# A two-layer language-model tower on one core: set-up steps, normalisation, context, causal mask and the first ternary layer rearranged

## The chip, the core and the metric

The kernel runs on one core of one Trainium2 chip. A core has five engines with instruction lists of their own: PE (TensorE, matrix products), DVE (VectorE), ACT (ScalarE), POOL (GpSimd) and SP (SyncE, which here only issues DMAs). They wait for one another through semaphores. SBUF is the on-chip memory of 128 partitions, PSUM the memory of eight banks into which TensorE writes. The metric is device time in microseconds.

## The reference

The input is 16 sequences of 128 tokens, hidden size 256, 16 heads of 16 features. Layer 0 embeds and normalises the tokens, applies attention with random features and then a low-rank mixture of prototypes. Layer 1 is causal attention with rotary embedding and a ternary feed-forward part. In short:

```
x  = layernorm(word[ids] + pos[types] + type[mask]) * gamma + beta
# layer 0, attention: 44 random features a head
td = (t * dn) @ proj.T
qp = ratio * (exp(td_q - diag_q - rowmax) + EPS)
kp = ratio * (exp(td_k - diag_k - max over keys and features) + EPS)
context = einsum('bhnm,bhnd->bhmd', kp, v)
out = einsum('bhmd,bhnm,bhn->bhnd', context, qp, 1 / (qp @ kp.sum))
h  = relu((out @ Wo.T + bo) @ Wfc.T + bfc), added to the stream
# layer 0, feed-forward: the two nearest of 32 prototypes, rank 16 each, gated
# layer 1, attention
q, k = rope(h @ Wq), rope(h @ Wk)
a  = softmax(causal(q @ k.T / 4)) @ v @ Wo
# layer 1, feed-forward: ternary weights
Wt = clip(round(W / (mean|W| + 1e-5)), -1, 1)
y  = relu(n(h) @ W1t.T + b1) @ W2t.T + b2
```

Every sublayer is fed a layernorm of the stream and added to it.

## The kernel before

One tile is one sequence (128 tokens on the partitions). There are 16 tiles, and each goes through some 90 named steps. A step is one or a few instructions on one engine, and it is written once, in that engine's `step(op, t)`. There is no loop over tiles in the usual sense: `due(engine)` sorts all (step, tile) pairs of an engine by a planned time, computed from `START`, `STRETCH` and `PLACE`, and the engine runs the sorted list in that order. About six to eight tiles are in flight: TensorE has issued the first product of tile 7 before the last one of tile 0. On TensorE the function `free` adds waits for the readers of a PSUM bank before the bank is written again.

Matrices are kept as a 16-bit upper part and a 16-bit lower part. `split_product` sums three products for each of the two halves of the contraction (L1320). Five layernorms a tile carry the letters E, P, F, R, M. For each, DVE makes the statistics (`Est`, `Eag` and so on), POOL raises to the power -1/2 (`Ers`, L539 and its like), DVE makes the negated mean times that (`Enm` L768, `Pnm` L785, `Fnm` L886, `Rnm` L956, `Mnm` L1018), and ACT normalises (`Exn` ..., L1075).

Steps that matter here, with their lines:

- *Start.* POOL writes constants (L601 to L626), gathers embedding rows (`g`, L521), adds them (`e2`, L535), scales and shifts (`esc` L542, `eh` L545). DVE fixes the ids first and writes padding (L1044 to L1062).
- *Set-up.* Loaded weights are split: ACT makes the upper part (L1078), DVE the lower (L659). These pieces are blocks inside the step of some tile: for example `setup_r` and `lower_rows("m")` stand behind `hg` of tile 0, `setup_f2` and `setup_masks` behind `on` of tile 0, and `quantise` (L749, L751), which makes the ternary weights, behind `kd` and `on` of tiles 1 and 2. The loads of later weights stand behind `qT` and `qp` of tile 0 on SP.
- *Context.* `ctx` (L1487) multiplies the key features of two heads (88 fp32 columns) with the values of two heads. The products across the two heads are not wanted: `ctxt` (L843) multiplies in PSUM by `pair_mask`, `cth` (ACT) and `ctl` (L846) split the result, and `o` (L1508) applies it to the queries. `kbc` (L1472) spreads the keys' maximum to all partitions.
- *Causal attention.* `mk1` and `mk2` (L1382) each write a mask of 0 and -1e30 into four PSUM banks: four matmuls of the identity with 512 columns. `s1` (L1737) adds the 16 heads' scores with tokens on partitions, `ngm` (L987) takes the negated row maximum, and `s2` (L1758) makes the transposed scores with the maximum as one more contraction row. `ex1` and `ex2` take the exponential and `pvx` (L1771) multiplies with the values, four heads side by side in the array's columns. Each score matmul has 48 rows of contraction of a head's 64 slots in `s1`, 64 in `s2`.
- *Feed-forward, layer 1.* `m1` (L1862, L1863) has tokens on partitions: eight matmuls of 512 columns and two for the bias. `mh1`, `mh2` (ACT, L1309, L1305) and `ml1`, `ml2` (DVE, L1030, L1026) split the result into `ms`, which lies over `stage_r`. It is transposed by a DMA (`mT`) for tiles 0 to 14, and on TensorE (`mTp` L1830, then `mTa`, `mTb`) for tile 15. `m2` (L1878, L1879) is the last product, `ob` (L1035) adds it to the stream and `st` stores it.

## Time and profile before

| | |
|---|---|
| three runs, us | 479.64, 479.53, 477.95 (median 479.53) |
| profiled execution (its time is known as its span) | 481.0 us |
| instructions | 11690 |
| PE, weight loads (PEld) | 82%, 56% of the span |
| DVE, ACT, POOL | 76%, 57%, 52% |
| mean granted TensorE clock | 0.929 of full speed |
| DMA moved | 56.47 MB |

All times in rows are microseconds from the start of the span unless ns is said. A row of a group reads: line, engine, operation, written tile `<-` read tiles, shapes, count, then busy time and the mean length of one in ns, then idle time of the engine just before and what ended it. A matmul row such as `128*88 128x34` has a stationary operand of 128 rows and 88 columns and streams 34 columns. Matmuls are pipelined: a run of equal ones is shorter than the sum of their lengths. An fp32 matmul is recorded twice.

### The profile page before, as it was taken

The numbers are of one execution on the slowest core, as the hardware profiler recorded it, in microseconds if no ns is written. First come the engines' busy times: TensorE is split into PE (matmuls) and PEld (weight loads), VectorE is DVE, ScalarE is ACT, GpSimd is POOL, SyncE is SP. The second block draws the span as 40 slices with busy tenths as digits, with TensorE's granted clock in tenths as the row PEclk, the third lists the DMA queues.
The fourth block names the chain that finished last, engine by engine and source line by source line (L and its number), as shares of the span: only waits on it lengthen the run. The fifth ranks groups of instructions, "written<-read, shape, count | busy, mean of one in ns | idle before, by whom it ended". The sixth has DMA issues, their size and how long they took to land. (4 is left out here: it accounts for less than half of the span.)

```text
span 481.0 us, 11690 instructions
## 1 busy us (share of the span) xinstructions
PE 395.6 (82%) x3871; PEld 268.2 (56%) x3901; DVE 367.2 (76%) x1009; ACT 273.6 (57%) x589; POOL 248.1 (52%) x334
## 2 busy tenths in 40 slices
PE   3263665787887899999999999999999989888876
PEld 1132443554555656667575757575757666565634
DVE  4466689988868888889888879798889786674552
ACT  1234673454747575858484857667575846455431
POOL 6883432565655656566666766656645434142000
PEclk9767557779989999999999999999999998999999
DMA  3928823043845657587989796979786963722223
GB/s 112 229 84 256 195 34 68 12 89 59 143 86 116 103 114 126 121 145 123 144 145 165 116 165 123 167 115 165 114 162 114 163 118 79 146 45 46 57 56 76
DMA packets 176908, 56.47 MB, mean 117 GB/s; under 512 B 168432, under 2 KB 174224, under 8 KB 176848
## 3 DMA queue, kind: packets, MB, share of 16 engines
q1 hardware_dynamic: 175216, 51.25, 57.3%
q0 software_dynamic: 1632, 4.46, 3.9%
q8 instruction: 32, 0.52, 0.5%
q14 instruction: 28, 0.23, 0.1%
HBM read 11.98 MB, written 2.36 MB: 30 GB/s over the span
## 5 line engine op out<-in xcount | busy, mean ns | idle before, releaser
L987 DVE TENSOR_REDUCE split<-PS 128x16 f16<-128x2048 f32 x16 | 36.8, 2297 | 5.9 <-PE PS L1737 5.6
L586 POOL TENSOR_TENSOR stage_f<-stage_f 128x512 f32<-128x512 f32 x16 | 20.2, 1265 | 33.4 <-DVE stage_f L965 27.3
L1075 ACT ACTIVATE xnR<-hres,nmeanR,rstdR 128x256 f32<-128x256 f32 x16 | 9.6, 600 | 43.7 <-DVE nmeanR L956 43.7
L1862 PE MATMUL PS<-w1q,xTM 128*128 128x512 f16 x128 | 32.8, 379 | 1.9 <-DMA xTM<-xsM 1.2
L1330 PE MATMUL PS<-proj_hi,qkT 128*128 128x176 f16 x128 | 24.3, 253 | 11.9 <-DMA qkT<-qs 9.1
L1878 PE MATMUL PS<-w2q,mT 128*128 128x256 f16 x256 | 30.6, 272 | 1.6 <-ACT mT L1072 0.9
L560 POOL TENSOR_TENSOR qe<-qef,qe 128x704 f16<-128x704 f32 x16 | 24.3, 1521 | 12.3 <-ACT qe L1165 12.3
L1878 PEld LDWEIGHTS PS<-w2q,mT 128*128 128x128 f16 x256 | 24.0, 98 | 5.9 <-issue 1.6
L1320 PE MATMUL PS<-wqkT_hi,xTP 128*128 128x512 f16 x64 | 24.5, 426 | 2.8 <-DVE proto_sq L683 2.5
L1620 PE MATMUL PS<-faT_hi,hgT 128*128 128x256 f16 x128 | 25.6, 288 | 1.3 <-DMA hgT<-hgs 0.8
L579 POOL TENSOR_TENSOR rstdR<-rstdR,consts 128x1 f32<-128x1 f32 x16 | 8.7, 546 | 33.3 <-DVE rstdR L952 33.3
L1075 ACT ACTIVATE ehat<-esum,nmeanE,rstdE 128x256 f32<-128x256 f32 x16 | 9.6, 598 | 28.4 <-DVE nmeanE L768 28.4
L1487 PEld LDWEIGHTS PS<-va,kp 128*88 128x88 f32 x256 | 24.0, 168 | 2.8 <-ACT kp L1172 0.6
L1072 ACT ACTIVATE split<-stage_f 128x256 f16<-128x256 f32 (+1 forms) x48 | 21.7, 477 | 5.2 <-POOL stage_f L586 4.7
L1331 PE MATMUL PS<-proj_lo,qkT 128*128 128x176 f16 x128 | 24.4, 253 | 0.0
L1487 PE MATMUL PS<-va,kp 128*88 128x34 f32 x256 | 23.9, 251 | 0.0
L1320 PE MATMUL PS<-rwqk_hi,xTR 128*128 128x512 f16 x64 | 21.8, 382 | 2.1 <-DVE xTR L960 1.4
L575 POOL TENSOR_TENSOR hgs<-hg,hgs 128x512 f16<-128x512 f32 x16 | 18.9, 1180 | 8.8 <-ACT hgs L1072 8.8
L1320 PE MATMUL PS<-fbT_hi,xTF 128*128 128x512 f16 x64 | 22.6, 394 | 0.0
L1330 PEld LDWEIGHTS PS<-proj_hi,qkT 128*128 128x128 f16 x128 | 13.2, 103 | 14.0 <-DMA qkT<-qs 10.3
L596 POOL TENSOR_TENSOR rstdM<-rstdM,consts 128x1 f32<-128x1 f32 x16 | 8.7, 542 | 23.7 <-DVE rstdM L1014 23.6
L555 POOL TENSOR_TENSOR xso<-onorm,xso 128x256 f16<-128x256 f32 x11 | 7.4, 670 | 26.0 <-ACT xso L1072 26.0
(324 smaller groups left out, 1405.5 us busy)
## 6 DMA issues: line engine op xcount, KB each, us to landing
out<-outb SPq DMA_DIRECT2D x16, 128.0 KB, 2.6
w<-in_w1T SPq DMA_DIRECT2D x1, 1024.0 KB
w<-in_w2T SPq DMA_DIRECT2D x1, 1024.0 KB
stage_p<-in_wqkT SPq DMA_DIRECT2D x1, 512.0 KB
stage_f<-in_fbT SPq DMA_DIRECT2D x1, 512.0 KB, 5.0
stage_f<-in_faT SPq DMA_DIRECT2D x1, 512.0 KB, 5.2
stage_r<-in_rwqk SPq DMA_DIRECT2D x1, 512.0 KB, 4.3
rT<-split SPq DMA_TRANSPOSE x26, 3.3
```

Source lines behind the costliest of these rows:

```text
L560: g.tensor_tensor(qel[:, :, 0:MP], pairs(qef), qeh[:, :, 0:MP], ALU.subtract).then_inc(qel_ok, 1)
L586: g.tensor_tensor(rot[:, :, :].rearrange("p h d -> p (h d)"), rc[:, :], rs[:, :], ALU.add).then_inc(rot_ok, 1)
L987: v.tensor_reduce(slots(48)[:, 0:H, 0].rearrange("p (c j) -> p j c", j=4), PS[:, BANK["mk1"]:BANK["mk1"] + 4, :].rearrange("p j (c k) -> p ...
L1072: return a.activation(dst, src, ACT.Copy)
L1075: a.activation(dst, src, ACT.Identity, bias=nmean[x][:, 0:1], scale=rstd[x][:, 1:2]).then_inc(xn_ok[x], 1)
L1320: last = pe.matmul(dst, xT[x][:, xp, :], wp[:, c, :], start=(n == 0), stop=(n == 3 * KC - 1 and bias is None))
L1330: pe.matmul(dst, qkT[:, c0 + c, :], proj_hi[:, :], start=True, stop=False)
L1331: last = pe.matmul(dst, qkT[:, c0 + c, :], proj_lo[:, :], start=False, stop=True)
L1487: last = pe.matmul(PS[0:MP, BANK["ctx"], 2 * VA * j:2 * VA * (j + 1)], kp[:, j * MP:(j + 1) * MP], va[:, 2 * j:2 * j + 2, :].rearrange("p ...
L1620: pe.matmul(PS[:, BANK["y"], 0:D], hgT[:, xp, :], wp[:, c, :], start=(c == 0 and xp == 0 and wp is whi["faT"]), stop=False)
L1862: pe.matmul(dst, xT["M"][:, n, :], w1q[:, n % KC, cols], start=(n == 0), stop=False)
L1878: pe.matmul(PS[:, BANK["m2"], 0:D], mT[:, j, :], w2q[:, j % FC, :], start=(j == 0), stop=False)
```

## The change

- *Order.* `due` no longer computes places. Each engine has a written list (`ORDER`), in which a step's n-th mention is its n-th tile. The warm-up products on TensorE and the choice of tiles that are turned by DMA stay.
- *Set-up apart.* The set-up blocks become pieces of their own in the lists (`zp1` ... `zq4` on DVE, `yp1` ... `ym3` on ACT, `xo1`, `xo2`, `xt` on TensorE, `lR`, `lW1`, `lW2` on SP). Scaling of the rope tables moves to the host. Constants other than the identity and the masks are written by DVE, ahead of its work on the ids; those left on POOL come ahead of its wait for the ids. In POOL's list the first steps are `g g e2 Ers esc e2 eh Prs Ers g e2 g` (before: `g g e2 Ers g esc e2 eh Ers Prs`).
- *Negated means.* The five `nmean` operations a tile move from DVE to POOL, right behind the power, with a wait for it.
- *Context.* Two heads get 64 feature slots each (128 instead of 88 columns), with zeros in the rest. `cth` and `ctl` read only the two diagonal blocks, each in two instructions of half the size, and apply the factor of `pair_mask`; `ctxt` and `pair_mask` go. `o` contracts over 128 rows.
- *Causal mask.* Scores come first in their banks. Up to 15 slots of a head that were empty now hold constants of +-6e4, which hide whole blocks of 32 tokens. Only the four diagonal 32 x 32 blocks of each bank get mask matmuls, behind the scores: 16 for `s1` and 16 for `s2`.
- *First ternary layer.* `m1` is written with features on partitions: 32 matmuls of 128 columns with the weights stationary, and the bias ahead of them, two matmuls of 64 rows. `mh` and `ml` write into `hidden` and `stage_r` in turn, and `m2` reads them there. `mT`, `mTp`, `mTa`, `mTb` go.

```
+                    g.wait_ge(rs_ok["R"], t + 1)
+                    g.tensor_scalar(nmean["R"][:, :], mv["R"][:, 0:1], rstd["R"][:, 1:2], -1.0, ALU.mult, ALU.mult)\
+                        .then_inc(nm_ok["R"], 1)
...
-                elif op == "ctxt":
-                    wait(v, ctx_ok, t + 1)
-                    ctxt = PS[0:MP, BANK["ctx"], 0:H * VA].rearrange("p (a b) -> p a b", a=HP)
-                    v.tensor_tensor(ctxt, ctxt, pair_mask[:, :, :], ALU.mult).then_inc(ctxt_ok, 1)
...
+                    for i in range(2):
+                        v.scalar_tensor_tensor(out=ctl[MS * i:MS * i + M, :, VA * i:VA * (i + 1)],
+                                               in0=diagonal(PS[:, BANK["ctx"], 0:H * VA], i), scalar=CS,
+                                               in1=cth[MS * i:MS * i + M, :, VA * i:VA * (i + 1)],
+                                               op0=ALU.mult, op1=ALU.subtract).then_inc(ctl_ok, 1)
...
+            for r in range(P // BLOCK - 1):
+                v.memset(queries[BLOCK * r:BLOCK * (r + 1), :, PARTS + FOLD * r:PARTS + FOLD * (r + 1)], HIDE).then_inc(pad_ok, 1)
+                v.memset(keys[BLOCK * (r + 1):BLOCK * (r + 2), :, PARTS:PARTS + FOLD * (r + 1)], -HIDE).then_inc(pad_ok, 1)
...
-            def masks(mask):
+            def hide(mask):
                 for j in range(4):
-                    pe.matmul(PS[:, BANK["mk1"] + j, :], ident_b[:, :], mask[:, :, :].rearrange("p c k -> p (c k)"),
-                              start=True, stop=False, skip_group_check=True)
+                    for r in range(P // BLOCK):
+                        block = slice(BLOCK * r, BLOCK * (r + 1))
+                        last = pe.matmul(PS[block, BANK["s1"] + j, :].rearrange("p (c k) -> p c k", c=4)[:, :, block],
+                                         ident_b[block, block], mask[block, block].unsqueeze(1).to_broadcast([BLOCK, 4, BLOCK]),
+                                         start=False, stop=True, skip_group_check=True, tile_position=(BLOCK * r, BLOCK * r))
+                return last
...
+                    for h in range(H):
+                        o = SLOT * (h % 2)
+                        pe.matmul(scores(h), rT[o:o + SLOT, HP + h // 2, :], rTm[o:o + SLOT, h // 2, :],
+                                  start=(h < 4), stop=False, skip_group_check=True)
+                    hide(mask_kq).then_inc(s2_ok, 1)
...
                     for b in range(2):
-                        dst = PS[:, BANK["m1"] + b, :]
-                        cols = slice(b * F1 // 2, (b + 1) * F1 // 2)
+                        pe.matmul(PS[:, BANK["m1"] + b, :], rows["m1"][0:BR, :], sel[:, 4 * b:4 * b + 4, :].rearrange("k c n -> k (c n)"),
+                                  start=True, stop=False, skip_group_check=True)
+                    for f in range(FC):
                         for n in range(2 * KC):
-                            pe.matmul(dst, xT["M"][:, n, :], w1q[:, n % KC, cols], start=(n == 0), stop=False)
-                        last = pe.matmul(dst, pick[:, :], rows["m"][:, cols], start=False, stop=True)
+                            last = pe.matmul(PS[:, BANK["m1"] + f // 4, f % 4 * P:(f % 4 + 1) * P], w1q[:, n % KC, f * P:(f + 1) * P],
+                                             xT["M"][:, n, :], start=False, stop=(n == 2 * KC - 1), skip_group_check=True)
                     last.then_inc(m1_ok, 1)
```

## Rows read from the trace of the kernel before

**Rows 1.** The page, busy us (share of the span) and instructions.
```profile
PE 395.6 (82%) x3871; PEld 268.2 (56%) x3901; DVE 367.2 (76%) x1009; ACT 273.6 (57%) x589; POOL 248.1 (52%) x334
```

**Rows 2.** Windows: stretch, its length, busy us by engine, clock, DMA share, GB/s.
```profile
64.00:112.00 48.00, 33.11 (x263) 22.46 (x263) 43.78 (x108) 21.73 (x51) 26.35 (x29) 0.73 0.27 54
203.60:409.40 205.80, 195.04 (x2061) 135.77 (x2078) 173.26 (x492) 137.28 (x306) 119.57 (x157) 0.99 0.80 136
```

**Rows 3.** Timeline (start, length, engine, line, operation): VectorE at the first output.
```profile
203.63 0.40 DVE L1035 SCALAR_TENSOR_TENSOR outb<-hres,PS 128x256 f32<-128x256 f32 x1
```

**Rows 4.** Timeline, TensorE, one tile's steps at full clock.
```profile
249.95 0.81 PE L1382 MATMUL PS<-mask_qk,ident_b 128*128 128x512 bf16 x3
250.69 0.62 PE L1737 MATMUL PS<-rT 48*128 48x128 f16 x16
...
259.38 0.39 PE L1472 MATMUL PS<-ident,kmx_row 16*128 16x16 f32 x2
259.83 1.08 PE L1771 MATMUL PS<-stage_p,vr 128*32 128x128 f32 x32
...
264.86 1.37 PE L1487 MATMUL PS<-va,kp 128*88 128x34 f32 x16
```

**Rows 5.** Groups by line and shape, TensorE (PE products, PEld weight loads).
```profile
L1487 PE MATMUL PS<-va,kp 128*88 128x34 f32 x256 | 23.9, 251 | 0.0
L1771 PE MATMUL PS<-stage_p,vr 128*32 128x128 f32 x512 | 18.1, 284 | 2.3 <-ACT stage_p L1271 1.7 <-issue 0.2
L1382 PE MATMUL PS<-mask_qk,ident_b 128*128 128x512 bf16 x48 | 12.9, 378 | 4.1 <-DVE rT L983 2.9 <-issue 0.5
L1737 PE MATMUL PS<-rT 48*128 48x128 f16 x256 | 10.0, 217 | 3.1 <-DMA rT<-split 3.1
L1472 PE MATMUL PS<-ident,kmx_row 16*128 16x16 f32 x32 | 6.5, 278 | 1.9 <-DVE kmx_row L827 1.9
L1771 PEld LDWEIGHTS PS<-stage_p,vr 128*32 128x32 f32 x512 | 14.0, 113 | 3.8 <-issue 3.4
```

**Rows 6.** Groups by line and shape, VectorE.
```profile
L843 DVE TENSOR_TENSOR PS<-PS,pair_mask 88x272 f32<-88x272 f32 x16 | 7.0, 436 | 2.2 <-PE PS L1487 2.2
L956 DVE TENSOR_SCALAR nmeanR<-mvR,rstdR 128x1 f32<-128x1 f32 x16 | 3.4, 211 | 1.6 <-POOL rstdR L579 1.6
```

**Rows 7.** Groups by line and shape, GpSimd.
```profile
L579 POOL TENSOR_TENSOR rstdR<-rstdR,consts 128x1 f32<-128x1 f32 x16 | 8.7, 546 | 33.3 <-DVE rstdR L952 33.3
L572 POOL TENSOR_TENSOR hgs<-gates,hgs 128x32 f16<-128x32 f32 x16 | 3.9, 245 | 5.6 <-ACT hgs L1072 5.5
```

**Rows 8.** Timeline of the first 32 us.
```profile
8.19 0.31 POOL L610 MEMSET fbias<- 32x256 f32 x1
...
11.71 0.98 POOL L521 DMA_INDIRECT hres<-in_word,ids  x1 [0.16 <-issue]
...
20.76 1.77 POOL L542 TENSOR_TENSOR escaled<-ehat,gamma 128x256 f32<-128x256 f32 x1
...
31.65 0.58 PE L1320 MATMUL PS<-wqkT_hi,xTP 128*128 128x512 f16 x1 [2.49 <-DVE proto_sq L683]
```

**Rows 9.** Timeline, VectorE: the steps on both sides of `setup_r` and `lower_rows("m")`.
```profile
77.13 0.69 DVE L922 SCALAR_TENSOR_TENSOR hg<-PS,gates 128x512 f32<-128x512 f32 x1
...
83.47 0.42 DVE L932 COPY hgT<-PS 128x512 f16<-128x512 f16 x1
```

**Rows 10.** The chain that ended last: start, length, what.
```profile
459.15 0.60 ACT stage_r L1309
...
459.78 0.69 DVE stage_r L1030
...
467.64 4.26 DMA mT<-stage_r
...
476.37 1.92 PE PS L1878 x16
```

**Rows 11.** Timeline, TensorE: the turn of the last tile, 16 blocks of 128 columns.
```profile
474.15 1.05 PE L1830 MATMUL PS<-ident_h,stage_r 128*128 128x128 f16 x16
```

More of the change, by code:

```diff
@@ L150, in taken, with made @@
     return op not in FOR_DMA or t not in BY_PE[FOR_DMA[op]]
-def due(engine):
-    def place(op, t):
-        return START[t] + STRETCH[t] * PLACE[op][0 if t < FIRST else 2 if t >= LAST else 1]
-    return sorted(((op, t) for op in ENGINE[engine] for t in range(TILES) if taken(op, t)), key=lambda x: (place(*x), x[1]))
-TURNS = {x: n + 1 for n, x in enumerate(y for y in due("PE") if y[0] in ("rT3p", "mTp", "rT1p", "rT2p", "hgTp",))}
+ONCE = {
[7 rows of a table added]
+}
+def due(engine):
+    seen = {}
+    for op in ORDER[engine].split():
+        tiles = [0] if op in ONCE[engine] else [t for t in range(TILES) if taken(op, t)]
+        n = seen[op] = seen.get(op, -1) + 1
+        yield op, tiles[n]
+def made(engine, piece, part=None):
+    count = 0
+    for op, _ in due(engine):
+        if op == piece:
+            return count + (ONCE[engine][op] if part is None else part)
+        count += ONCE[engine].get(op, 0)
+    raise KeyError(piece)
+TURNS = {x: n + 1 for n, x in enumerate(y for y in due("PE") if y[0] in ("rT3p", "rT1p", "rT2p", "hgTp"))}
 def wait(eng, sem, count):
@@ L972, in step @@
                 elif op == "rc":
+                    if t == 0:
+                        v.wait_ge(load["R"], 16 * 5)
                     wait(v, rqk_ok, t + 1)
@@ L1106, in setup_m, with upper_matrix @@
-            def setup_m():
-                a.wait_ge(load["M"], 16 * 3)
-                a.wait_ge(v_set, 10)
-                junk = wneg[:, :].bitcast(F16)
-                for k, w in enumerate((w1, w2)):
-                    a.wait_ge(a_set, 13 + k)
-                    a.activation(junk, w[:, :], ACT.Abs, accum_out=absum[:, k:k + 1]).then_inc(a_set, 1)
-                upper(rows["m"][0:BR, :], row["m"][:, :], 1.0)
+            def upper_matrix(src, k):
+                upper(whi[k][:, :, :], src[:, :, :], WS)
@@ L1171, in step @@
                     wait(a, ctx_ok, t)
-                    a.activation(kp[:, :], ke[:, :], ACT.Identity, bias=FEATURE_EPS).then_inc(kp_ok, 1)
+                    a.activation(kp[:, :, 0:M], by_feature(ke), ACT.Identity, bias=FEATURE_EPS).then_inc(kp_ok, 1)
                 elif op == "cth":
-                    wait(a, ctxt_ok, t + 1)
+                    wait(a, ctx_ok, t + 1)
                     wait(a, o_ok, t)
-                    copy(cth[:, :, :], PS[0:MP, BANK["ctx"], 0:H * VA].rearrange("p (a b) -> p a b", a=HP)).then_inc(cth_ok, 1)
-                    if t == 0:
-                        setup_r()
+                    for i in range(2):
+                        a.activation(cth[MS * i:MS * i + M, :, VA * i:VA * (i + 1)], diagonal(PS[:, BANK["ctx"], 0:H * VA], i),
+                                     ACT.Copy, scale=CS).then_inc(cth_ok, 1)
                 elif op == "oe":
```

986 lines of the change are left out of this document (531 added, 455 removed), and 39 rows, old and new, of tables (BANK, BY_PE, FOR_DMA, FOR_PE).

## The prediction, made before the changed kernel was run

> **What bounds the kernel now.** I read the page first: TensorE's matmul side is busy 82% of the span [rows 1]. Such averages hide stages, so next I read busy time by stretch, with stretches cut at events [rows 2]. The first output eviction is at 203.6 and the tenth at 409.4: nine tiles in 205.8 us, 22.87 us a tile. TensorE is busy 195.0 of them at full clock, VectorE 173.3 [rows 2, 3]. This stage is TensorE's. From 64 to 112 VectorE is busy 43.8 of 48.0 us and TensorE 33.1, at a mean clock of 0.73 [rows 2]: there VectorE's list is the limit, because one-off set-up stands between the steps of the first tiles [rows 9]. Before 31.65 TensorE has no tile's product at all [rows 8]. At the end I read the chain of waits: a DMA of 4.26 us and turns stand between the last products [rows 10].
>
> TensorE's records overlap, so I count pitches: (length of a run of n equal matmuls minus one of them) over n-1.
>
> **Part 1, the start.** *Gathers and constants.* Today GpSimd writes constants from 8.19 on, between the first tile's gathers and the second's (11.71), issues the second's, and only then makes the first sum; the third tile's gathers stand ahead of `esc` at 20.76 [rows 8]. Afterwards the constants are VectorE's (14 memsets, ahead of the ids) or come ahead of the ids on GpSimd, so the second tile's gathers and the sum move up by 11.71 - 8.19 = 3.5 us, and `esc` has no gather ahead of it: two of about 1 us each. `esc` of tile 0 also takes 1.77 us, beside a VectorE split; if the split moves, 1 us goes. VectorE's extra memsets can delay the ids a little, and the padding memsets delay the warm-up, where TensorE has no work yet. The first product needs the q/k weights too; their DMAs are released by the same event as now, and no row shows when they land. I take 7 us off 31.65. Bounds: 3.5 (the gathers alone) and 9.
>
> *Set-up apart.* Nothing of it but the rope scaling is removed; each piece gets a place of its own. Today 6.3 us of set-up stand between the gated product of tile 0 (77.13) and VectorE's next step of a tile (83.47) [rows 9], and the steps behind them queue. Ahead of tile 0's negated maximum (`ngm`), today's list has 14 negated means and three `ctxt`, which go: 14 x 0.21 + 3 x 0.44 = 4.2 us [rows 6]. Rope scaling, narrower masks and a shorter row add an estimated 1.9; three split `ctl` take 0.5 back. VectorE is contiguous there, so about 6 us. The moved pieces can as well land ahead of something urgent (in the new list three stand between `kd` and `ctl` of tile 0, a fourth just ahead of `kd`), so the bounds are 1 and 9. Start in all: 13 us, bounds 4.5 and 18.
>
> **Part 2, TensorE per tile.** *Causal mask.* Eight 512-column matmuls with the full identity go. Their pitch is (0.81-0.38)/2 = 0.216 us, so 1.73 us [rows 4, 5]. In come 32 matmuls of 32 rows, 32 weight columns and 128 moving columns, on the four diagonal blocks of the array. The extra contraction rows that hide whole blocks ride inside the score matmuls at no cost: 16 of those take 0.62 at 48 rows [rows 4], and their number and columns stay. No row shows a diagonal block. Nearest: the half-height scores, two side by side, pitch (0.62-0.22)/15 = 0.027, and the quarter-width `pvx`, four side by side, (1.08-0.28)/31 = 0.026 a record, fp32 [rows 4, 5]. I take 0.027: 0.86 us, a saving of 0.87. Lower bound, four abreast, 0.0135: saves 1.30. Upper bound, one at a time, (1.05-0.22)/15 = 0.055 as in the last turn [rows 11]: 1.76, no saving. Beyond that lies rival C.
>
> The Trainium skill speaks against the saving. Its page "TensorEngine Tiling (Array Packing)", section "Gotcha 1: PSUM Pressure", says that different row tiles cannot write the same PSUM bank at the same time. Here four do; today's score pairs go to different banks. By it the masks would cost the upper bound, which is rival B.
>
> *Context.* A head's features get 64 slots, not 44, so `ctx` loads 128 fp32 weight columns, not 88. Its pitch today is (1.37-0.25)/15 = 0.075 for 34 moving columns, more than `pvx` needs for 128, so the load sets it. The `kbc` matmul loads 128 fp32 columns for 16 moving ones: two in 0.39 with 0.28 each, a pitch of 0.11 [rows 4, 5]. Cost 16 x (0.11-0.075) = 0.57 us; bounds 0 and 0.57.
>
> The Trainium skill agrees: "TensorE: Matmul & The Clock Gate", section "LDWEIGHTS (loading the stationary operand)", has the load grow with weight columns and not with rows.
>
> *First ternary layer.* Eight 512-column matmuls of 0.216 become 32 of 128 at 0.055 [rows 11], 1.73 to 1.76; the two bias matmuls stay. The features land on partitions, so the transposed copy `mT` (15 DMAs, one turn on TensorE) disappears.
>
> Per tile -0.87 + 0.57 + 0.03 = -0.27; over 16 tiles -4 us, bounds -20 (masks four abreast, context free) and +10 (masks singly, context dear).
>
> **Part 3, the other engines.** VectorE loses five negated means (1.05) and `ctxt` (0.44) a tile and gains at most 0.2 for `ctl` in two halves: -1.3 us [rows 6]. GpSimd gains five small operations, each between the 0.25 of `gsl` and the 0.55 of its power [rows 7]: 1.3 to 2.8 us a tile, on an engine that is idle half of the time; its place in line is that of the power. Queued behind it are `esc`, `Plo`, `qel`; ScalarE's normalisation waits for it, up to 0.4 later than today, hidden while TensorE has other tiles. ScalarE gets `cth` twice, 0.2. Of TensorE's 10.8 idle us in the nine tiles [rows 2] some are waits for VectorE; its freed time and a new order can close or open gaps. I take -2 over the run, from -8 to +5. The `mT` DMAs free queue time that nobody waits for before the end: nothing.
>
> **Part 4, the end.** Today the last product starts at 476.37: ahead of it stand tile 14's DMA (4.26 from 467.64), its product, a turn of 16 blocks and its copies [rows 10]. The last first layer has run by about 471.4, since tile 14's product follows the DMA at once. Afterwards a ScalarE eviction (0.60) and two VectorE ones (0.69 each, overlapping by a little) lead from it to the product, as they lead to the DMA today: 0.60 + 2 x 0.69 = 2.0 [rows 10]. So 473.5, 2.9 earlier. Masks on the chain give 0.5, the mean on GpSimd takes some back. -3, bounds -1 and -5.
>
> **Sum.** The profiled span is 481.0; the median of the three runs is 1.5 less. 481.0 - 13 - 4 - 2 - 3 = 459.0, less 1.5 = **457.5 us**. Start and end carry 16 of the 22.
>
> **Rivals.**
> A. *The start keeps only the gathers' part* (4.5 instead of 13): the moved set-up stands ahead of the first tiles' chain. 466. For it: the four pieces named above, and on ScalarE three matrix splits ahead of tile 0's `ke`. Against: VectorE's list is shorter whatever its order.
> B. *Mask matmuls run singly*, being in one bank: 0.90 us a tile more than taken, 457.5 + 14 = 472. Against: they differ in output partitions as well, and `pvx` shares its bank.
> C. *The slow side: the small blocks' weight loads don't hide, or the array empties at each change of shape.* A load of 32 columns is recorded at 0.113 us in `pvx`, hidden there [rows 5]. At that a matmul the masks cost 3.6 a tile, 2.75 more than taken: 457.5 + 44 = 502. It makes the kernel slower than now from 22/16 = 1.4 us more than taken, that is from 2.25/32 = 0.07 us a matmul. Against: `pvx` and the scores hide theirs.
> D. *Masks four abreast and gaps closing:* 457.5 - 7 - 6 = 444.
>
> **How the numbers follow.** Forecast (448 to 465) 0.56, A 0.14, B 0.14, C 0.08, D 0.05, and 0.03 that the new order costs what the rest gives (about 480). The range takes in D and B, with a margin for A and B in part together: 443 to 476. A measurement of this kernel tells about 0.5% from no change. Faster by more: 0.86; within: 0.05; slower: 0.09.
>
> **What would show it.** First q/k product near 24; `ngm` of tile 0 near 99 instead of 112; outputs 22.4 to 22.7 apart; 16 mask matmuls in about 0.4 us behind 16 scores; 16 `ctx` records in about 1.9 instead of 1.37; the last product about 2 us behind the last first layer. The prediction is wrong if the outputs are 22.9 or more apart, or the first comes no earlier than 195.

## The result and the profile after

The changed kernel takes 488.0 us (median of five runs, 483.2 to 489.6) beside 478.2 for the kernel before (five runs, 475.8 to 479.6): a ratio of 1.021, 95% interval 1.017 to 1.025. The prediction was 457.5 us, range 443 to 476, and both signs that it named for being wrong are there: outputs 22.9 or more apart (23.12) and a first output no earlier than 195 (205.1). It has the wrong sign. Ratios are formed without executions of a slower state, which matters for e16 at the end of the table: it stands on four of ten, and over all ten it would be 1.014. The span of the profiled execution, 481.3 us, is the shortest of the five and hardly differs from that before (481.0), so I read the parts of the profile first and then a second profile of the same kernel (span 488.5, on another chip, where the ratio was 1.015).

The line of busy times of the page of the kernel after, and then its busy time by stretch (columns as in [rows 2]):

```profile
PE 395.1 (82%) x4653; PEld 288.2 (60%) x4653; DVE 353.6 (73%) x947; ACT 275.8 (57%) x605; POOL 270.8 (56%) x401
```

```profile
64.00:110.00 46.00, 35.56 (x271) 23.71 (x269) 38.21 (x91) 25.93 (x57) 26.55 (x32) 0.72 0.29 58
205.10:413.20 208.10, 191.61 (x2470) 144.02 (x2468) 164.90 (x446) 139.39 (x315) 125.41 (x190) 0.99 0.64 111
413.20:481.30 68.10, 55.04 (x747) 41.14 (x747) 36.16 (x89) 28.99 (x59) 13.24 (x22) 1.00 0.12 31
```

From the first output (205.10) to the tenth (413.18) lie 208.1 us, 23.12 a tile, where it was 22.87 [rows 2, 3]. TensorE is busy 191.6 us of it, not 195.0: its work did fall, by 0.38 us a tile. But it stands idle 16.5 us instead of 10.8. VectorE is busy 164.9 instead of 173.3 and GpSimd 125.4 instead of 119.6. Both moved the way that the change says (VectorE by 0.93 us a tile where 1.3 was forecast, GpSimd by 0.65 for 1.3 to 2.8), and the tiles came no closer.

Times from the trace, kernel before against kernel after:

| | before | after |
|---|---|---|
| first q/k product | 31.65 | 25.42 |
| first negated maximum | 112.1 | 110.4 |
| first output | 203.6 | 205.1 |
| tenth output | 409.4 | 413.2 |
| last output | 478.4 | 478.8 |

The way from the first negated maximum to the first output, in which the pipeline fills, took 94.7 us instead of 91.5. The prediction did not look at this stretch by itself, and it costs more than the nine tiles behind it (3.2 against 2.3 us).

TensorE's timeline of the kernel after, one tile at full clock (columns: start, length, engine, line, operation and tiles, form, count). L1825 is the first score products, L1458 the block masks, L1847 the second score products, L1859 `pvx`, L1579 `ctx`, L1930 and L1934 the bias and weights of `m1`:

```profile
251.86 0.62 PE L1825 MATMUL PS<-rT 63*128 63x128 f16 x16
252.41 0.40 PE L1458 MATMUL PS<-mask_qk,ident_b 32*32 32x128 bf16 x16
252.75 0.28 PE L1392 MATMUL PS<-rwv_hi,xTR 128*128 128x256 f16 x1
...
258.80 0.62 PE L1847 MATMUL PS<-rTm,rT 64*128 64x128 f16 x16
259.35 0.40 PE L1458 MATMUL PS<-mask_kq,ident_b 32*32 32x128 bf16 x16
...
261.93 1.08 PE L1859 MATMUL PS<-stage_p,vr 128*32 128x128 f32 x32 [0.23 <-issue]
...
264.67 1.95 PE L1579 MATMUL PS<-va,kp 128*128 128x34 f32 x16
266.45 0.63 PE L1873 MATMUL PS<-ident,stage_f 128*128 128x128 f32 x4
...
268.31 0.60 PE L1930 MATMUL PS<-sel,rows_all 64*128 64x512 f16 x2
268.85 1.96 PE L1934 MATMUL PS<-xTM,w1q 128*128 128x128 f16 x32
270.64 0.24 PE L1402 MATMUL PS<-proj_hi,qkT 128*128 128x176 f16 x1
```

The prices of the sum can be read off. The 16 masks keep TensorE from 252.41 to 252.75, 0.34 us: twice that is 0.68 a tile, less than the 0.86 I took and half-way to the lower bound. `ctx` lasts 1.95 where 1.9 was forecast. From its start to the next step are 1.78 us; before, 1.20 (264.86 to 266.06; its record is in [rows 4]). `m1` takes 268.31 to 270.64, 2.33 us; before it was ten records at a pitch of 0.216, 2.16: +0.17 where I took +0.03. Together -1.05 + 0.58 + 0.17 = -0.30 against a forecast of -0.27 and a measured fall of 0.38.

The rows show one more thing, which the sum did not hold. The second scores start 6.94 us behind the first (258.80 - 251.86) and `pvx` 3.13 behind them. In the kernel before the same tile's `pvx` starts at 259.83, 9.14 behind the first scores [rows 4]; now it is 10.07.

What TensorE waited for in the nine tiles of the kernel after (waiting line, releaser, us in total, times, longest):

```profile
PE PS L1392 <- DMA xTo<-xso: 2.0, 4, 0.9
PE PS L1551 <- DVE kmx L883: 2.0, 3, 1.0
PE PS L1564 <- DVE kmx_row L887: 1.8, 4, 0.5
PE PS L1859 <- ACT stage_p L1343: 1.8, 3, 0.7
PE PS L1825 <- DMA rT<-split: 1.6, 2, 1.3
```

No single wait has appeared. The idle time is spread over a dozen of them, each below 1.4 us.

### The profile page after: what moved, and what is told of

Its sections match the earlier page's. It is cut to its first block, busy times and chain, and to the rows that moved or that the text cites. A ratio compares the mean times of both kernels' runs of the same rounds, so it can differ in the third digit from the quotient of the medians.

```text
span 481.3 us, 13220 instructions
## 1 busy us (share of the span) xinstructions
PE 395.1 (82%) x4653; PEld 288.2 (60%) x4653; DVE 353.6 (73%) x947; ACT 275.8 (57%) x605; POOL 270.8 (56%) x401
## 4 chain that ended last, share of the span: by engine, by line
PE 43%; issue 12%; DVE 12%; POOL 11%; DMA 10%; ACT 7%; SPq 3%; ACTq 0%; POOLq 0%; DVEq 0%
PE PS L1392 12%; PE PS L1579 4%; PE PS L1934 4%; DMA rT<-split 4%; PE PS L1859 3%; PE PS L1952 3%; DMA xTo<-xso 2%; PE PS L1710 2%; DMA hgT<-hgs 2%; PE PS L1458 1%; SPq L508 1%; POOL emb L566 1%; PE PS L1930 1%; PE PS L1402 1%; POOL split L656 1%
## 5 line engine op out<-in xcount | busy, mean ns | idle before, releaser
L1579 PE MATMUL PS<-va,kp 128*128 128x34 f32 x256 | 33.7, 290 | 3.4 <-ACT kp L1246 3.3
L1579 PEld LDWEIGHTS PS<-va,kp 128*128 128x128 f32 x256 | 33.2, 208 | 5.3 <-ACT kp L1246 4.5
L1934 PEld LDWEIGHTS PS<-xTM,w1q 128*128 128x128 f16 x512 | 28.6, 98 | 6.8 <-issue 6.8
L1934 PE MATMUL PS<-xTM,w1q 128*128 128x128 f16 x512 | 31.4, 219 | 0.0
L1710 PE MATMUL PS<-faT_hi,hgT 128*128 128x256 f16 x128 | 27.4, 300 | 1.9 <-DMA hgT<-hgs 1.4
L1392 PE MATMUL PS<-rwqk_hi,xTR 128*128 128x512 f16 x64 | 23.2, 405 | 0.4 <-DVE xTR L1003 0.3
L1133 ACT ACTIVATE ehat<-esum,nmeanE,rstdE 128x256 f32<-128x256 f32 x16 | 9.5, 593 | 21.9 <-POOL nmeanE L593 21.1
L656 POOL TENSOR_TENSOR split<-stage_f,split 128x512 f16<-128x512 f32 x16 | 18.5, 1155 | 5.5 <-ACT split L1130 5.4
L1859 PE MATMUL PS<-stage_p,vr 128*32 128x128 f32 x512 | 17.6, 278 | 3.4 <-ACT stage_p L1343 1.8
L566 POOL DMA_INDIRECT hres<-in_word,ids x16 | 16.9, 1054 | 5.8 <-DVE ids_pt L1103 2.9
L1392 PE MATMUL PS<-wvT_hi,xTP 128*128 128x256 f16 x64 | 14.6, 294 | 6.5 <-DVE wvT_lo L716 6.5
```

Of the source, the lines that this page charges most:

```text
L566: g.indirect_dma_start(dst, None, table, bass.IndirectOffsetOnAxis(rows_, 0)).then_inc(g_ok[slot], 16)
L656: g.tensor_tensor(slots(32), rot[:, :, :], slots(16), ALU.subtract).then_inc(rl_ok, 1)
L1392: last = pe.matmul(dst, xT[x][:, xp, :], wp[:, c, :], start=(n == 0), stop=(n == 3 * KC - 1 and bias is None))
L1579: last = pe.matmul(PS[:, BANK["ctx"], 2 * VA * j:2 * VA * (j + 1)], kp[:, 2 * j:2 * j + 2, :].rearrange("p h m -> p (h m)"), va[:, 2 * j:2 ...
L1710: pe.matmul(PS[:, BANK["y"], 0:D], hgT[:, xp, :], wp[:, c, :], start=(c == 0 and xp == 0 and wp is whi["faT"]), stop=False)
L1859: last = pe.matmul(PS[32 * j:32 * (j + 1), BANK["pvx"], c * P:(c + 1) * P], vr[:, 4 * c + j, :], pfull[:, j, c, :], start=True, stop=True)
```

## The experiments

The lists of both kernels hold the same tile steps, so orders and parts can be exchanged. For the runs on the **old order** the place function of the kernel before was evaluated, its steps written out as lists, and the set-up pieces put behind the steps that carried them before. Each ratio is to the kernel before on the same chip. Spacing is the mean distance of outputs one to ten in the profile, busy is TensorE's time in these nine tiles over nine, idle the rest.

| run | ratio (95% interval) | spacing | busy | idle |
|---|---|---|---|---|
| before (its own profile) | 1 | 22.87 | 21.67 | 1.20 |
| after | 1.021 (1.017 to 1.025) | 23.12 | 21.29 | 1.83 |
| e1 after, again | 1.015 (1.011 to 1.019) | 23.48 | 21.17 | 2.31 |
| e2 old order | 1.037 (1.032 to 1.041) | 23.75 | 21.39 | 2.37 |
| e3 old order, new set-up | 1.071 (1.066 to 1.075) | 23.71 | 21.39 | 2.32 |
| e4 new order, old set-up | 1.034 (1.028 to 1.041) | 23.49 | 21.33 | 2.16 |
| e5 e2 + means on VectorE | 1.020 (1.013 to 1.026) | 23.21 | 21.16 | 2.05 |
| e6 e2 + old masks | 1.007 (1.003 to 1.011) | 23.27 | 22.10 | 1.17 |
| e9 e2 + small masks ahead | 1.013 (1.008 to 1.017) | 23.30 | 21.56 | 1.74 |
| e7 e6 + means + 108 columns | 0.997 (0.993 to 1.001) | 22.89 | 21.93 | 0.96 |
| e10 e7, both masks small | 1.005 (1.001 to 1.009) | 23.29 | 21.51 | 1.77 |
| e13 e7, first mask small | 1.001 (0.996 to 1.005) | 22.67 | 21.38 | 1.29 |
| e14 e7, second mask small | 1.004 (1.001 to 1.008) | 23.27 | 21.76 | 1.50 |
| e17 e13, half of GpSimd's work | 0.996 (0.993 to 0.999) | 22.84 | 21.55 | 1.30 |
| e18 e13, half of the maximum | 0.996 (0.993 to 0.999) | 22.25 | 21.35 | 0.90 |
| e8 after, 108 columns | 1.007 (1.003 to 1.011) | 22.92 | 21.02 | 1.90 |
| e11 after, means on VectorE | 1.020 (1.011 to 1.030) | 23.25 | 21.28 | 1.97 |
| e12 after, small masks ahead | 1.012 (1.007 to 1.017) | 23.20 | 21.30 | 1.90 |
| e15 after, start moved | 1.010 (1.003 to 1.018) | | | |
| e16 e12 + 108 columns + start | 1.005 (0.999 to 1.011) | | | |

The profiled execution of e15 took 490.4 us beside 482.9 to 484.8 for its four others, and that of e16 485.4 beside a median of 484.4, so only the order of events is read in them. e17 and e18 leave out work and are no candidates.

### Order or work (e1 to e4)

My first theory was that the new lists had lost what the new work gained; the rival was that the new work itself opens the gaps.

e1, the changed kernel again:

> The changed kernel itself, for comparison with the three orders beside it. From its five times, 483.2 to 489.6 us, median 488.0, a ratio to the kernel before of about 1.02. Its own profile (span 481.3) stands at the low end of its times; this look is to show where the other runs lose some 5 us more: if it is one stall, one stretch between outputs is longer than in the first profile; if it is many gaps, the nine tiles from the first to the tenth output take 210 to 213 us rather than 208.1.

Measured 1.015; the nine tiles took 211.3 us, spread as expected. The longest distances between outputs stand at the same places in both profiles (the third, 25.1 and 26.1 us, and the seventh, 26.3 and 26.2); the first six together are longer in e1 by 3.6 us. The same kernel's spacing differs by 0.36 us between the two profiles, so below the ratios decide, and a spacing from one profile only supports them.

e2, old order, all the new work:

> All of the changed work (masks by rows and blocks, means on GpSimd, wide context, feature-major layer), but each engine's tile steps in the order of the kernel before, and the set-up pieces behind the same steps as before. Theory ORDER (the new lists lose what the new work gains): 461 to 470 us, outputs 22.4 to 22.8 us apart, first output near 198. Theory WORK (a part of the new work, such as the wait for GpSimd's mean or the wide context, opens TensorE's gaps whatever the order): 480 to 490, outputs 23.0 or more apart.

```
-ORDER = { ... the new lists ... }
+ORDER = { ... the kernel before's steps in its order, set-up behind the steps that held it ... }
```

Measured 1.037, 500.6 us, outputs 23.75 apart. ORDER fell: the new lists are better for the new work than the old ones are, by 2%. It is not one stage: the first output comes at 212.5 instead of 208.8 (e1), and the outputs are 0.27 us further apart.

e3 and e4 exchange the places of the set-up only:

> As the run with the old order, but the set-up pieces stand where the new lists have them (ahead of the same or a neighbouring tile step). If the new place of the set-up is what costs the start, this is slower than the old order by 3 to 6 us, with the first context product of tile 0 near 52 as in the changed kernel; if the place of the set-up is worth the 6 us that the prediction gave it, it is faster by 3 to 6.

> The changed kernel with its tile steps in the new order, but the set-up pieces behind the same steps as before. Under the theory that the set-up's new place costs: 482 to 485 us. Under the theory that the order of the tile steps costs: within 1% of the changed kernel, 485 to 493, and outputs still 23 us or more apart.

Both lost: 1.071 from 1.037, and 1.034 from 1.015. The first negated maximum came at 129.6 instead of 113.0, and at 121.2 instead of 114.5. A place of the set-up is worth up to 3% of the run, but neither place is better in itself. Each fits its own tile order. Part of it can be the clock: TensorE was granted its lower level, 1.2 GHz, for 85.1 us ahead of the first maximum in e3 and for 51.6 in e2, for 69.9 in e4 and for 62.4 in e1.

### The parts, on the old order (e5, e6, e7)

e5 takes the negated mean out of GpSimd's steps and puts it at its old place in VectorE's list:

```
-                    g.wait_ge(rs_ok["R"], t + 1)
-                    g.tensor_scalar(nmean["R"][:, :], ...)
+    "DVE": ... Rag hP Pst Rnm ...
```

> The old-order run (500.6 us beside a kernel before of 482.4, outputs 23.75 us apart) with the five negated means a tile back on VectorE at their old places. If the wait for GpSimd's second operation is what spreads the outputs: about 485 us. If the cause is elsewhere: within 3 us of 500.6, or slower by up to 5, since VectorE gets 1.05 us a tile back.

Measured 1.020 from 1.037, although VectorE got the five means back (its busy time rose by 0.58 us a tile, from 167.9 to 173.1 us in the nine tiles; GpSimd's fell by 1.27). On that order GpSimd was the worse place for the means. Most of the gain lies ahead of the nine tiles: the first output comes at 202.4 instead of 212.5.

e6 puts four full mask matmuls ahead of the scores, as own steps, in place of the blocks behind them:

```
-                    hide(mask_qk).then_inc(s1_ok, 1)
+                elif op == "mk1": ... 4 x matmul(identity, 128 x 512) ...
+                elif op == "s1": ... scores only ...
```

> The old-order run with the four 512-column mask matmuls ahead of the scores at their old places, in their own steps, and none of the block masks (the hiding rows hold zeros, so the result is the same). TensorE gets about 1.0 us a tile of work back. By the sum of TensorE's work this is slower than 500.6 by up to 16 us. If it is the masks behind the scores, on the way from scores to the negated maximum and to the exponentials, that hold the tile up, with four banks held meanwhile, it is no slower or faster: 485 to 500.

Measured 1.007 from 1.037: the kernel became 3% faster with 0.7 us a tile more to do on TensorE (22.10 busy for 21.39). This is the opposite of what the sum of TensorE's work says. Here too more than half lies ahead of the first output (201.0 instead of 212.5), and part can be the granted clock, of which more below.

e7 has both, and a context product of 108 columns:

```
-                        ... kp[:, 2 * j:2 * j + 2, :]  (128 columns)
+                        ... kp[:, 2 * j:2 * j + 2, :] ... [:, 0:MS + M]  (108 columns)
```

> The old-order run with three parts back: means on VectorE, old masks, and 108 instead of 128 weight columns in the context product (rows 108 to 127 of its output are read by nobody). If these three are what differs in effect from the kernel before, about 482 to 486 us. If it stays near 500, the cause is in what is left: the feature-major first layer with its later release of banks, the context split in halves, or the changed start.

Measured 0.997: as fast as the kernel before. So on the old order the three parts together make the loss; what is left (feature-major layer, context in halves and 20 columns wider, the start's constants) sums to nothing that can be measured. That they make it on the new order too is not shown by this; e8, e11 and e12 ask it.

### The place of the masks and their size (e9, e10, e13, e14)

> The old-order run with the small block masks issued ahead of the scores, as steps at the old masks' places, and the hiding rows kept: only the place of the masks differs from the old-order run (1.037 of the kernel before), only their shape and the hiding rows from the run with the old masks (1.007). Theory PLACE (masks behind the scores lengthen the way from scores to maximum and exponentials and leave TensorE nothing to do in its waits): 1.007 or less, by up to 1.0 us a tile of TensorE's work, 466 to 482 us. Theory SHAPE (the small blocks themselves disturb): stays near 1.037, 496 us.

e9 has the small blocks of the changed kernel, but issues them ahead of the scores (`start=True` in the blocks, `start=False` in the scores). Measured 1.013 from 1.037: PLACE accounts for most of the 3% that e6 gave back. In the trace the maximum starts 0.60 us behind the start of the last score product in e2 and 0.27 in e9 (mean of tiles 5 to 13), and the exponentials 0.60 and 0.27 behind the last second score. In the kernel before they are 0.28 and 0.26. Behind the scores, each group of masks stands on the way of its own tile, for 0.33 us. But e9 is not faster than e6 (1.007), which has 0.54 us more TensorE work.

> As the run before it, and means on VectorE and 108 weight columns. The same with the old masks took 0.997 of the kernel before. Theory PLACE: 0.965 to 0.99, 461 to 474 us, since 1.0 us a tile of TensorE's work goes. If TensorE's work no longer sets the time there: 0.997.

Measured 1.005: with cheaper masks than e7 it is, if anything, slower. Here are the nine tiles of e7, then of e10, then of e13, and behind them the stretch from the first maximum to the first output in e7 and in e10 (columns as in [rows 2]):

```profile
196.10:402.10 206.00, 197.36 (x2295) 146.64 (x2294) 173.04 (x492) 140.67 (x315) 119.84 (x158) 1.00 0.65 114
```

```profile
201.50:411.10 209.60, 193.63 (x2520) 144.64 (x2516) 172.80 (x493) 139.96 (x315) 119.79 (x158) 0.98 0.64 111
```

```profile
197.40:401.40 204.00, 192.40 (x2396) 144.60 (x2394) 173.10 (x492) 139.93 (x315) 119.97 (x158) 1.00 0.64 115
```

```profile
108.70:196.10 87.40, 78.67 (x894) 56.29 (x892) 75.34 (x221) 60.44 (x137) 52.52 (x67) 1.00 0.59 110
109.90:201.50 91.60, 79.83 (x986) 57.06 (x987) 75.67 (x221) 60.61 (x137) 52.53 (x67) 0.95 0.66 105
```

TensorE can be busy 197.4 us of 206.0 at full clock. With 3.7 us less to do, it needs 209.6. So its work at full clock did not set the time in e10. But the granted clock there was 0.98 instead of 1.00, and ahead of the first output 0.95 instead of 1.00, and this is a rival to every explanation by waits. The time that TensorE stood at its lower level, 1.2 GHz, between the first maximum and the last output:

| | first maximum to last output, us | of it at 1.2 GHz, us |
|---|---|---|
| before | 366.3 | 6.8 |
| after | 368.3 | 10.2 |
| e1 | 371.4 | 5.8 |
| e2 | 383.2 | 20.1 |
| e6 | 365.5 | 3.0 |
| e9 | 368.5 | 12.9 |
| e7 | 360.3 | 0 |
| e10 | 368.9 | 23.3 |
| e13 | 362.1 | 9.6 |
| e14 | 367.3 | 13.7 |

What such time costs can be read at either level: `pvx` takes 1.94 us in e10 at 396.89, at the lower level, and 1.08 in [rows 4]. As an estimate from the two levels, a microsecond at 1.2 GHz loses at most half of itself. So e10 can owe the clock up to 11.7 us, more than the 8.6 by which it is longer than e7, and e14 up to 6.9 of its 7.0: waits and clock are not separated there. The ten executions of e10 say the same: the five shortest (478.5 to 480.2 us) were granted 0.928 to 0.936 of full speed in the mean, the five others (480.4 to 483.9) 0.915 to 0.922. Ahead of the fall at 396.0 in e10 TensorE had been busy 5.30 of 6.8 us. No run shows whether the saved work brings the fall about. Other differences are too large for the clock: e9 is 14.7 us shorter than e2, the clock can be 3.6 of it, and e6 is 17.7 shorter, the clock 8.6. And it does not explain the loss of the changed kernel, which in e1 stood at the lower level for less time than the kernel before.

e13 and e14 make one mask small and leave the other full:

> Old order, means on VectorE, 108 weight columns, masks ahead: the mask of the first scores as 16 small blocks, that of the second as four full matmuls. With both full the ratio was 0.997, with both small 1.005. Theory COVER (the stretch from first to second scores is as long as the maximum and a transposing DMA take, so that TensorE's work saved in it is lost, and only work saved outside it counts): 0.5 us a tile faster than both full, ratio 0.975 to 0.99, the stretch near 6.5 us, the rest of a tile near 13.1. If neither half counts: 0.997 to 1.005.

> The mirror of the run before: full masks ahead of the first scores, small ones ahead of the second. Theory COVER: no faster than both full (0.997), up to 1.5% slower, with the stretch from first to second scores near 7.2 us instead of 6.5 and TensorE idle over 1 us in it. If saved work counts wherever it is: the same as the run before.

Measured 1.001 and 1.004: neither half is worth anything that the times show. The theory COVER is half right at most. I cut each tile on TensorE at the first of the first scores, the first of the second scores and `pvx` (mean of tiles 5 to 12, which leave out the ends of the nine tiles, where e14 and most of e10 lose their clock; us, idle time in brackets):

| | first to second scores | to `pvx` | to the next first scores |
|---|---|---|---|
| before | 6.46 (0.37) | 2.86 | 13.71 (0.48) |
| e2 | 7.10 (1.40) | 3.21 | 13.62 (0.56) |
| e7 | 6.49 (0.40) | 2.88 | 13.67 (0.06) |
| e10 | 7.20 (1.40) | 3.00 | 13.03 (0.00) |
| e13 | 6.97 (0.86) | 2.86 | 13.10 (0.05) |
| e14 | 6.61 (0.93) | 2.88 | 13.65 (0.04) |
| after | 7.22 (1.01) | 4.36 | 12.38 (0.30) |

A cheap second mask (e14) leaves TensorE idle 0.5 us longer in the first stretch: as COVER says, the full mask had only filled a wait. A cheap first mask (e13) does shorten the last stretch, by 0.57 us. But then the first stretch is 0.48 longer, idle again. The saving becomes a wait, and the rows of what TensorE waited for from 200 to 400 us say for what, first in e13:

```profile
PE PS L1386 <- DMA xTo<-xso: 4.3, 6, 1.4
PE PS L1858 <- DMA rTm<-split: 2.3, 5, 0.7
```

In e7 no wait for `xTo` is listed, and that for `rTm` is as long:

```profile
PE PS L1850 <- DMA rTm<-split: 2.5, 2, 1.4
```

So it is not the operand of the second scores (`rTm`) that comes late in e13, but `xTo`, the transposed attention output of layer 0, which the product `of` in the same stretch needs. GpSimd makes its lower part and SP issues its DMA.

### What holds the tiles then (e17, e18)

> The run with the first mask cheap (ratio 1.001, outputs 22.67 us apart), with GpSimd's three longest operations (lower part of the query features, sum of the rotated halves, lower part of the gated product) halved in tiles 1 to 15; the other half of their outputs keeps old values. GpSimd loses about 2.0 us a tile. If GpSimd's list holds the tiles: the issue of the DMA for the second scores comes at once behind the maximum (0.47 us late before), the outputs come closer by 0.5 to 1.2 us, ratio 0.965 to 0.985. If not: ratio and spacing unchanged.

e17 leaves out half of GpSimd's three longest operations. Measured 0.996 from 1.001: 1.7 us less GpSimd work a tile (busy 104.7 for 120.0 us in the nine tiles) gave some 2 us in the whole run, with intervals that overlap. The wait for `xTo` fell from 4.3 to 1.9 us, and that for `rTm` rose from 2.3 to 4.4. GpSimd's list alone does not hold the tiles.

> The run with the first mask cheap, with the negated maximum taken for 8 of 16 heads in tiles 1 to 15 (the other heads keep the tile before's). The way from first to second scores gets 1.15 us shorter, and VectorE's list too. If that way holds the tiles: the stretch from first to second scores falls from 6.97 to about 6.1, where TensorE's own work of it ends, the outputs come closer by 0.8 us, ratio 0.96 to 0.975. If GpSimd's list or another holds them: the outputs stay 22.5 to 22.7 apart, and TensorE's idle time moves elsewhere.

e18 takes the maximum of 8 of the 16 heads only. Measured 0.996 too (against 1.001, again with overlapping intervals), with outputs 22.25 apart. The way from first to second scores was shortened by 1.07 us (2.30 to 1.23), and the stretch by 0.33 (6.97 to 6.64). The rows of one tile say why: SP's issues of the three transposing DMAs that stand together in its list (`onT`, `roT`, `rT3`), and VectorE's maximum, first in e13:

```profile
289.42 1.19 SPq L525 DMA_TRANSPOSE xTo<-xso  x1
289.54 2.30 DVE L1030 TENSOR_REDUCE split<-PS 128x16 f16<-128x2048 f32 x1
291.04 1.31 SPq L529 DMA_TRANSPOSE xTr<-xsr  x1
292.44 1.25 SPq L521 DMA_TRANSPOSE rTm<-split  x1
```

and in e18:

```profile
288.94 1.19 SPq L525 DMA_TRANSPOSE xTo<-xso  x1
289.06 1.23 DVE L1031 TENSOR_REDUCE split<-PS 128x8 f16<-128x1024 f32 x1
290.57 1.19 SPq L529 DMA_TRANSPOSE xTr<-xsr  x1
291.86 1.25 SPq L521 DMA_TRANSPOSE rTm<-split  x1
```

In e13 the maximum ends at 291.84 and `rTm` is issued at 292.44, when SP is done with `xTr` at 292.35. In e18 the maximum ends at 290.29, and the issue still comes at 291.86, behind `xTr` (291.76). An issue of a transposing DMA takes SP 1.2 to 1.3 us here, and `xTo` comes when GpSimd has made its lower part. In e7 (mean of tiles 5 to 13) the maximum ends 0.78 us after SP is done with the issue ahead, in e13 0.11 and in e18 0.85 before it. So I read one way (scores, maximum, DMA) as held by another (output of layer 0's attention, GpSimd, SP's queue) as soon as it gets shorter; no run moves `rTm` ahead in SP's list, which would test it.

The Trainium skill, page "TensorEngine Tiling (Array Packing)", section "Gotcha 1: PSUM Pressure", was weighed against the masks in the prediction; the trace does not bear it out here: four row tiles write one bank with a pitch of (0.40 - 0.22)/15 = 0.012 us, where one at a time had 0.055 [rows 11].

### The new order (e8, e11, e12)

> The changed kernel with 108 instead of 128 weight columns in the context product, the least that its slots allow. The pitch was 0.075 us at 88 columns and 0.111 at 128, so 16 records should take about 0.29 us a tile less: 4.6 us over the run if TensorE's work sets the time (485 us), nothing if waits set it.

Measured 1.007 against 1.015 for e1 (and 1.021 for the five runs): 0.8 to 1.4%, with 1.0 expected. The intervals of e8 and e1 just miss each other. Of TensorE's prices this is the one that shows in the time: twenty columns of the forty added are worth about 5 us.

> The changed kernel with the negated means back on VectorE, each at the place in VectorE's list at which GpSimd made it in the profile. In the old order this gave 1.7% back. If GpSimd's longer queue is the cause in any order: about 1.000 to 1.005 of the kernel before, 480 us. If the new lists have hidden it: no change from 1.015 to 1.021, or a little slower.

Measured 1.020 (1.011 to 1.030): no change from 1.015 to 1.021 that can be seen. The new lists seem to hide the means on GpSimd, which cost 1.7% on the old order.

> The changed kernel with the block masks ahead of the scores: for the first scores directly ahead of them, for the second three steps ahead (there they wait for the maximum). Theory PLACE: faster than the changed kernel by 1 to 3%. If the new lists have already fitted the rest around the masks behind: within 1% of it; slower if the earlier wait for the maximum now holds the three steps between.

Measured 1.012; the interval overlaps that of e1, so a gain of up to 1% is likely, not shown.

### The start (e15), and all together (e16)

In the kernel after, TensorE's first tile (timeline; in brackets idle time ahead and what ended it) and the step of ScalarE that held it:

```profile
25.42 0.58 PE L1392 MATMUL PS<-wqkT_hi,xTP 128*128 128x512 f16 x1 [1.49 <-DVE xTP L854]
...
36.80 0.40 PE L1392 MATMUL PS<-wvT_hi,xTP 128*128 128x256 f16 x1 [6.48 <-DVE wvT_lo L716]
...
41.80 0.31 PE L1402 MATMUL PS<-proj_hi,qkT 128*128 128x176 f16 x1 [2.37 <-DVE qd L875]
...
52.18 3.48 PE L1579 MATMUL PS<-va,kp 128*128 128x34 f32 x16 [3.13 <-ACT kp L1246]
```

```profile
34.63 0.60 ACT L1133 ACTIVATE ehat<-esum,nmeanE,rstdE 128x256 f32<-128x256 f32 x1 [5.43 <-POOL nmeanE L593]
35.13 0.61 ACT L1136 ACTIVATE wvT_hi<-stage_p 128x512 f16<-128x512 f32 x1
```

The first product is 6.2 us earlier than before, but the first context product, at 52.18, is 1.8 us later than the 50.34 of the kernel before. The split of the value weights stands behind the third tile's normalisation, which waits for its negated mean from GpSimd, behind that tile's gather.

```
-ACT: ... qhi0 Exn2 yp2 sq0 va0 ...         DVE: ... qlo0 Est2 Eag2 zm zo1 Pst1 Pag1 zp2 Est3 diag0 ...
+ACT: ... qhi0 yp2 sq0 Exn2 va0 ...         DVE: ... qlo0 zp2 Est2 Eag2 zm zo1 Pst1 Pag1 Est3 diag0 ...
```

> The changed kernel with three entries moved for tile 0: on ScalarE the upper part of the value weights and the squares ahead of the third tile's first normalisation, on VectorE the lower part of the value weights ahead of the third tile's statistics. In the profile ScalarE stood 5.4 us ahead of that normalisation and TensorE 6.5 us for the value weights. If this is what ate the start's gain: value product of tile 0 near 31 instead of 36.8, first negated maximum 3 to 5 us earlier than 110.4 to 114.5, time 1.010 of the kernel before instead of 1.018. If VectorE's list holds the start further on whatever comes in: the first negated maximum moves by under 1 us, time unchanged.

TensorE and then VectorE in e15:

```profile
31.27 0.27 PE L1398 MATMUL PS<-wvT_hi,xTP 128*128 128x256 f16 x1
...
43.23 0.30 PE L1408 MATMUL PS<-proj_hi,qkT 128*128 128x176 f16 x1 [9.11 <-DVE qd L881]
```

```profile
36.23 0.43 DVE L846 BATCH_NORM_STATS2 statsP<-hres 128x6 f32<-128x256 f32 x1 [2.21 <-POOL hres L609]
...
39.98 0.43 DVE L832 BATCH_NORM_STATS2 statsE<-esum 128x6 f32<-128x256 f32 x1 [2.93 <-POOL esum L593]
40.33 0.67 DVE L868 TENSOR_REDUCE diag<-sq 128x32 f32<-128x512 f32 x1
```

The value product came 5.5 us earlier, as the first theory said, and the next product of keys no earlier, as its rival said: VectorE stands at the statistics of tiles 1 and 3, which wait for GpSimd's sums, and tile 0's own steps are queued behind them. The first context product comes at 56.1, later than in both profiles of the changed kernel (52.2 and 55.3), and the first maximum at 113.7, between theirs. The time, 1.010, lies below 1.015 to 1.021, with intervals that overlap.

> The changed kernel with the small masks ahead of the scores (alone 1.012), 108 weight columns (alone 1.007) and the three moved entries. If they add up from 1.018: about 0.994, or 0.99 with the full gain of the start.

Measured 1.005 (0.999 to 1.011), where the single gains add up to 0.994. Its executions lie between 476.6 and 487.5 us, so this is the least certain value of the table. No version of mine is measurably faster than the kernel before and does all of its work; e7 comes closest.

## Why the prediction was wrong, step by step

Against the forecast of 22 us less, the two profiles miss by this much, stage by stage:

| | forecast | after | e1 |
|---|---|---|---|
| up to the first maximum | -13 | -1.7 | +2.3 |
| from there to the first output | in the terms per tile | +3.2 | +2.9 |
| nine tiles | -3.4 (9 of 16 tiles of -4 and -2) | +2.3 | +5.5 |
| tenth to last output | -3 | -3.4 | -3.3 |

So two steps failed: the start is the largest miss in microseconds, and what bounds the tiles is the one that gave the wrong sign.

**What bounds the kernel** is the step that failed in the tiles. I read "TensorE is busy 195.0 of 205.8 us at full clock" as "this stage is TensorE's" and turned each saved microsecond of it into time. The table above refutes the second half: busy time ran from 21.0 to 22.1 us a tile over the runs, and the spacing did not follow it. As far as e13, e17 and e18 show, several ways around a tile are within some 2% of each other: TensorE's list, the way scores, maximum, DMA, second scores, and the way over GpSimd and SP's queue. The wait rows of the kernel before held a hint that I had read as small change: 1.3 us for `rTm` and 1.7 for `pvx` in nine tiles, at the very places from which the change took the masks.

**Causal mask.** The price was right, even on the low side (0.68 us for 0.86). That the saving is time was wrong: on the old order full masks ahead are as fast as small ones ahead (1.007 and 1.013). What I did not cost at all is the new place. Part of the masks' work had lain under waits (that of the second scores, e14), and behind the scores it lies on the tile's way: 1.013 against 1.037 on the old order, about 11 us. On the new order moving the masks gave at most 1% (e12), so there the place is not shown to be the cause. Rival C had the sign, but another mechanism, at a price per matmul (0.07 us) that the runs exclude; rival B is excluded too (0.012 where it had 0.055).

**Context.** The 0.57 us a tile were right (0.58), and they are the one price that shows in the time about in full: 108 columns for 128 give back about 1% of the run (e8). Bounds of 0 and 0.57 hid that this gets worse than the gain beside it, if only the gain is covered.

**First ternary layer.** +0.17 instead of +0.03, mostly the bias matmuls with 64 rows (0.54 for 0.43). That removing 15 DMAs gives nothing before the end fits e7, which is no faster than the kernel before; no run tests it alone.

**Means on GpSimd.** Forecast as hidden. On the new order that holds as far as e11 shows, on the old one it cost 1.7% (e5). "Idle half of the time" said nothing on what is queued there.

**Gaps.** I took -2 us over the run from a range of -8 to +5. In the nine tiles alone TensorE's idle time rose by 5.7 us in one profile and about 10 in the other. This term was mis-sized and had the wrong sign: work taken away from TensorE left the waits standing. It also left out the granted clock, which e10 shows can take back a saving.

**Start.** The second step that failed, the term of 13 us. First product at 25.4 instead of 31.7: 6.2 of the 7 us came. They were gone by the first maximum (1.7 left of 13; in e1 it came 2.3 later than before). The 6 us for the set-up did not come either: e3 and e4 show that its place costs or gives according to the order of the tile steps around it. Rival A described this, with its four pieces, but stopped at 4.5 us. The trace of e15 puts the loss down above all to the statistics of later tiles in VectorE's list, behind GpSimd's gathers; no run moved these, so this cause is read and not tested.

**End.** From the tenth to the last output 65.6 us instead of 69.0: -3.4, forecast -3. The last first layer ends at 473.93 and the last product starts at 476.69, 2.8 us behind it (forecast 2); no DMA or turn is left between.

So -3.4 at the end, a first output 1.5 to 5.2 us later where 13 or more earlier was forecast, and 0.25 to 0.62 us a tile more in between. The two spans that were profiled are 481.3 and 488.5; they differ in both stretches, and why is left open.

## To carry over

In a pipeline of fixed lists, a busy engine is not yet the bound. Before pricing a saving, cut the tile at the points where the engine meets another's result, and ask of each stretch whether the engine's own work or the other's way is longer; work removed from a stretch that another's way fills is worth nothing, and work moved behind a result lengthens that way. Here a wider operand counted in the time while a saving of the same size beside it did not: sum such terms apart, not against each other. Compare the granted clock of two profiles before a wait is blamed for their difference. And an order fits the work it was made for: when one is changed, the other has to be measured anew.

## What the chip showed beyond that

Sixteen 32 x 32 products with 128 moving columns on the four diagonal blocks, four to a PSUM bank, start 0.012 us apart. The records of fp32 products of 34 moving columns follow one another at 0.11 us with 128 weight columns and at 0.075 with 88. The issue of one transposing DMA holds SP's queue for 1.2 to 1.3 us (1.8 to 2.5 in a few cases), so three that stand together take some 3.8 us there, more than the 3.3 that one takes from issue to landing (median of `rTm`). Where TensorE had more to do (e7, 21.9 us a tile busy) it was granted 1.00 of its clock in the nine tiles, where it had less and idled more (e10) 0.98; e6 and e9, with 3.0 and 12.9 us at 1.2 GHz from the first maximum to the last output, point the same way, and e13 and e14 stand between. These are single profiles, and whether the idle time is the cause is not shown.
